# Carrying a routing gate as a 513th column of its dispatched row, in an attention and mixture-of-experts kernel

## The reference, cut to what matters

```python
probs = jax.nn.softmax(xt @ Wg, axis=-1)
gate = jnp.take_along_axis(probs, eidx[:, None], 1)[:, 0]
flat = jnp.where(keep, eidx * C + pos, E * C)
xd = jnp.zeros((E * C, d), x.dtype).at[flat].set(xt, mode='drop')
...
out = jnp.take(oe, jnp.minimum(flat, E * C - 1), axis=0)
out = out * (gate * keep.astype(x.dtype))[:, None]
out + shared
```

## Time and profile before

| | |
|---|---|
| median of 3 runs | 1058.2 us (1057.88 to 1059.21) |
| span of the profiled execution, first to last instruction | 1056.1 us |
| time of its own of that execution | not listed apart; the median stands 2.1 us above its span |
| PE busy | 1028.1 us, 97% of the span |
| DVE, ACT, POOL busy | 726.8, 551.9, 545.2 us |
| PE's share of the chain that ended last | 89% |
| granted clock of TensorE, mean | 0.996 |

### The profile page before, as it was taken

One profiled execution on the slowest core, in us unless ns is written; L12 is line 12 of the kernel. 1 busy time (PEld: TensorE's weight loads), 2 busy tenths in 40 slices (PEclk: granted clock), 3 DMA queues, 4 the chain that ended last, 5 costly groups with the idle time before them and its releaser, 6 DMA issues.

```text
span 1056.1 us, 16138 instructions
## 1 busy us (share of the span) xinstructions
PE 1028.1 (97%) x5570; PEld 720.2 (68%) x5570; DVE 726.8 (69%) x1206; ACT 551.9 (52%) x970; POOL 545.2 (52%) x309
## 2 busy tenths in 40 slices
PE   5999999999999999999999999999999999999996
PEld 5877556465564655545545568788899999998884
DVE  4549877878788788887888568723666666663164
ACT  3321565656666566665665663512455666663116
POOL 2200688988888988889888863173000000004500
PEclk9999999999999999999999999999999999999998
DMA  8945441444316253241353456372477777775604
GB/s 266 321 127 154 111 100 51 103 109 120 101 51 156 56 134 86 60 121 32 90 180 110 140 160 199 92 212 60 111 213 222 213 228 222 233 211 109 96 1 159
DMA packets 162181, 145.74 MB, mean 138 GB/s; under 512 B 42481, under 2 KB 125681, under 8 KB 161856
## 3 DMA queue, kind: packets, MB, share of 16 engines
q1 hardware_dynamic: 154720, 128.62, 43.8%
q0 software_dynamic: 6656, 15.93, 5.4%
q10 hardware_dynamic: 736, 0.30, 0.1%
HBM read 84.70 MB, written 35.67 MB: 114 GB/s over the span
## 4 chain that ended last, share of the span: by engine, by line
PE 89%; DVE 4%; DMA 2%; ACT 2%; issue 1%; SPq 0%; ACTq 0%; DVEq 0%
PE bank L829 20%; PE bank L987 13%; PE bank L1000 12%; PE bank L935 12%; PE bank L1137 10%; PE bank L923 8%; PE bank L1045 4%; PE bank L895 3%; PE bank L1012 3%; PE bank L836 2%; DVE mx L1648 1%; DMA raw<-in_L_ffn_W_dram 1%; PE bank L1114 1%; DMA lora_c<-in_L_attn_Ao_dram 1%; PE bank L868 1%
## 5 line engine op out<-in xcount | busy, mean ns | idle before, releaser
L1377 ACT ACTIVATE prob<-bank 128x512 f32<-128x512 f32 x512 | 290.1, 597 | 188.0 <-PE bank L987 180.0
L1648 DVE TENSOR_REDUCE mx<-bank 128x1 f32<-128x512 f32 x512 | 325.0, 679 | 75.4 <-PE bank L935 72.3
L758 POOL TENSOR_TENSOR psum<-psum,prob 128x1024 f32<-128x1024 f32 x156 | 366.8, 2392 | 0.0
L987 PE MATMUL bank<-Qs,Ks 97*128 97x512 f32 x512 | 208.7, 423 | 0.9 <-DMA Qs<-mrow 0.9
L935 PE MATMUL bank<-Ks,Qs 96*128 96x512 f32 x512 | 184.6, 405 | 2.9 <-DVE mx L1648 1.3
L987 PEld LDWEIGHTS bank<-Qs,Ks 97*128 97x128 f32 x512 | 94.2, 188 | 106.2 <-ACT prob L1377 74.3
L1000 PE MATMUL bank<-prob,V 128*32 128x512 f32 x1024 | 131.4, 602 | 0.0
L935 PEld LDWEIGHTS bank<-Ks,Qs 96*128 96x128 f32 x512 | 97.0, 189 | 49.3 <-DVE mx L1648 21.9
L808 POOL DMA_DIRECT2D oe_d<-oe_sb x16 | 8.7, 546 | 228.6 <-ACT oe_sb L1514 227.6
L758 POOL TENSOR_TENSOR psum<-prob,prob 128x1024 f32<-128x1024 f32 x32 | 76.1, 2399 | 62.7 <-ACT prob L1377 33.6
L923 PE MATMUL bank<-xThi,Wsl 128*128 128x512 f32 x256 | 98.4, 396 | 0.8 <-DVE plane_klo L1638 0.8
(11 more groups left out here) (257 smaller groups left out, 2075.7 us busy)
## 6 DMA issues: line engine op xcount, KB each, us to landing
raw<-in_L_ffn_W_dram SPq DMA_DIRECT2D x120, 256.0 KB, 3.6
Ks<-plane_khi SPq DMA_DIRECT2D x64, 128.0 KB, 2.5
Qs<-plane_qhi SPq DMA_DIRECT2D x64, 128.0 KB, 2.3
raw<-in_L_ffn_sw_dram SPq DMA_DIRECT2D x30, 256.0 KB, 4.0
xin<-in_L_attn_x_dram SPq DMA_DIRECT2D x16, 256.0 KB, 5.8
v_d<-v_sb POOLq DMA_DIRECT2D x16, 256.0 KB, 3.6
Ks<-plane_klo SPq DMA_DIRECT2D x32, 128.0 KB, 2.6
Qs<-plane_qlo SPq DMA_DIRECT2D x32, 128.0 KB, 2.3
```

What stands on the lines that cost most here:

```text
L758: po.tensor_tensor(psum[:, pr], (prob[0] if kc == 1 else psum)[:, pr], prob[kc % RING][:, pr], ALU.add).then_inc(sem("sum_done"), 1)
L987: nc.tensor.matmul(score_at(v, i), Ks[v.b][0:97, hh, kc * P:(kc + 1) * P], Qs[v.b][0:97, hh, v.hf * HALF:(v.hf + 1) * HALF], start=True, s ...
L1377: ACTV(prob[kc % RING][:, hh, :], score_at(v, i), ACT.Exp, scale=SCALE).then_inc(sem("exp_done"), 1)
L1648: ins = RED(mx[(hf + ahead) % 2][:, 4 * hh + qt, part:part + 1], src, AX.X, ALU.max)
```

## The change

`xd_d` gets rows of 513 elements (2052 bytes) instead of 512, and so do `rows_a` and `rows_b`. The reciprocal writes the gate into element 512 of each row, in two instructions, one for each buffer. The 16 row stores then carry the gate along; the 16 stores of gates, the table `gate_d`, its clear and two waits go. The clear of `xd_d` goes in pieces of 57 elements (228 bytes) instead of 64 (256 bytes). The slot loads read 512 of 513 elements of each row, and the gates are loaded from column 512 of `xd_d`. All users of the rows as tokens get a view of their first 512 elements. The attention stage's buffers, and with them most of the second stage's, begin 32 bytes later than before (`rows_b` now on a multiple of 64 bytes; the two `w13` buffers behind it, and everything in `late`, 64 bytes later), and the small routing buffers behind the removed gate buffer 32 bytes earlier.

```diff
+ROW = D + 1
...
-    xd_d = nc.dram_tensor("xd_d", [E * CAP, D], F32).ap()
-    gate_d = nc.dram_tensor("gate_d", [E * CAP, 1], F32).ap()
+    xd_d = nc.dram_tensor("xd_d", [E * CAP, ROW], F32).ap()
...
-    region = keep.at
+    region = keep.at + 4 * NT // 2
...
-    early = Arena(nc, region, small_at - V_BYTES)
-    rows_a = early("rows_a", [P, NT // 2, D], F32)
+    early = Arena(nc, keep.at, small_at - V_BYTES)
+    rows_a = early("rows_a", [P, NT // 2, ROW], F32)
...
-    wide = Arena(nc, overlay, sum_at)
-    rows_b = wide("rows_b", [P, NT // 2, D], F32)
+    wide = Arena(nc, overlay, sum_at + 4 * NT // 2)
+    rows_b = wide("rows_b", [P, NT // 2, ROW], F32)
...
-    late = Arena(nc, sum_at, nc.sbuf_usable_end)
+    late = Arena(nc, wide.at, nc.sbuf_usable_end)
...
     def rows(t):
+        return gated_rows(t)[:, 0:D]
+
+    def gated_rows(t):
         return (rows_a if t < NT // 2 else rows_b)[:, t % (NT // 2)]
...
-                sp.dma_start(gate_d.rearrange("(p n) o -> p (n o)", p=P), zeros[:, 0:E * CAP // P]).then_inc(sem("gate_zero"), 16)
...
-            sp.dma_start(xd_d.rearrange("(p n) (a b) -> p (n a) b", p=P, a=8)[:, i * n * 8:(i + 1) * n * 8, :],
-                         zeros[:].unsqueeze(1).to_broadcast([P, n * 8, D // 8])).then_inc(sem("xd_zero"), 16)
+            sp.dma_start(xd_d.rearrange("(p n) (a b) -> p (n a) b", p=P, a=9)[:, i * n * 9:(i + 1) * n * 9, :],
+                         zeros[:, 0:ROW // 9].unsqueeze(1).to_broadcast([P, n * 9, ROW // 9])).then_inc(sem("xd_zero"), 16)
...
-                sp.dma_start(xdi[j][:], xd_d[bass.ds(r, P), :]).then_inc(sem(f"xd_ld{j}"), 16)
+                sp.dma_start(xdi[j][:], xd_d[bass.ds(r, P), 0:D]).then_inc(sem(f"xd_ld{j}"), 16)
...
-        sp.wait_ge(sem("gate_put"), 16 * NT)
-        sp.dma_start(gate_sb[:], gate_d.rearrange("(n p) o -> p (n o)", p=P),
+        sp.dma_start(gate_sb[:], xd_d[:, D:ROW].rearrange("(n p) o -> p (n o)", p=P),
                      allow_slow_non_contiguous=True).then_inc(sem("gate_ld"), 16)
...
-                                  in_=rows(t), in_offset=None, bounds_check=E * CAP - 1,
+                                  in_=gated_rows(t), in_offset=None, bounds_check=E * CAP - 1,
                                   oob_is_err=False).then_inc(sem(f"scat{t // 4}"), 16)
-
-        po.wait_ge(sem("gate_zero"), 16)
-        for t in range(NT):
-            po.indirect_dma_start(out=gate_d, out_offset=bass.IndirectOffsetOnAxis(ap=sidx[:, t:t + 1], axis=0),
-                                  in_=r2["gate"][:, t:t + 1], in_offset=None, bounds_check=E * CAP - 1,
-                                  oob_is_err=False).then_inc(sem("gate_put"), 16)
...
-        link(nc.vector.reciprocal(r2["gate"][:], r2["sm"][:]))
+        for k, part in enumerate((rows_a, rows_b)):
+            link(nc.vector.reciprocal(part[:, :, D], r2["sm"][:, k * NT // 2:(k + 1) * NT // 2]))
```

More of the change, by code:

```diff
@@ L331, in emit @@
     r3 = {n: mid(f"r3_{n}", [P, NT, E], F32) for n in ("lg", "d", "ex", "c", "oh", "s0", "s1", "io")}
-    r2 = {n: mid(f"r2_{n}", [P, NT], F32) for n in ("mx", "sm", "gate", "em", "ps", "keep", "flat", "t")}
+    r2 = {n: mid(f"r2_{n}", [P, NT], F32) for n in ("mx", "sm", "em", "ps", "keep", "flat", "t")}
     tri = mid("tri", [P, P], BF16)
```

## The result

The changed kernel takes 1085.88 us (median of 4 runs, 1082.74 to 1089.92), the kernel before beside it 1058.04 us (4 runs, 1057.29 to 1059.21). The ratio is 1.0263, interval 1.0245 to 1.0281: slower by 27.8 us, where "no difference" was forecast and 1060.5 was the upper end.

What follows compares the result with a forecast made beforehand. PE, busy 97% of the span, was taken as the bound, the gate stores as a cost nobody pays. Six zeros and +0.1 us on the last output store took 1058.2 to 1058.3 us, "no difference"; range 1056.8 to 1060.5.

Steps and rivals of the forecast that it cites:

- The clear goes in more and odder pieces: Clear of the slot table: lands after 13 to 15 us instead of 11.3, hidden by 20.7 us of cover; 0.
- PE waiting for `Qs<-mrow`: Attention stage: with a clear of over 20.7 us, named as a sign that the forecast is wrong.
- The gate stores go: POOL, 703.45 to 724.53 us: some 21 us freed, but ScalarE sets POOL's next work; 0.
- Rival A: Gate stores disturbed something, sharing DMA engines with weight loads: 1057.0 us at best; gain over 0.2% given 0.04.
- The row stores: 16 stores of 2052 bytes a row: bytes grow 0.2%, a store may come 19 us late; 0.
- the reciprocals: DVE's chain: two of about 0.20 us, 0.18 us more in all, hidden by 0.24 us idling; 0 to +0.2.
- the gate load: Gates read from places 2052 bytes apart: landed after 4.3 us before, some 37 us of cover; 0.
- the slot loads: Expert stage, 16 loads of 256 KB at 4.5 us from rows 2052 bytes apart: a little longer is absorbed; 0.
- rival B: Expert stage: slot loads with odd starts delay each expert's weight loads; 2.1 us at 6%, 4.2 at 12%; chance 0.06.
- POOL's idle time: After POOL's last store at about 703 us: idles some 83 us instead of 62.
- the output stores: Tail: four stores, the last landing after 2.1 us; +0.1 us for the 4-byte offset, between 0 and +0.3.
- the shift by 32 bytes: All buffers, attention stage above all: engines don't mind 32 bytes; 0, with +/-1 us of uncertainty.

Runs made afterwards that it cites:

- the fourth group: Last of four groups of follow-up runs, each with the kernel before at its side; here that took 1057.4 us (21 runs), going by its time without stalls.
- three other groups: The first three groups of follow-up runs, where the kernel before took 1079.51, 1078.18 and 1078.10 us.
- the paced version: Kernel before with two waits of POOL inside its 32 indirect stores, before the first and ninth gate store: 1061.24 us, ratio 0.9839.
- the clear mended: Changed kernel with only the slot table's clear altered, to 192-byte pieces starting on multiples of 64: 1061.34 us, ratio 0.9828.
- the pauses: Two waits of POOL inside the sixteen row stores, added to the changed kernel with 192-byte clear pieces: 1057.65 us, ratio 0.9810.
- the two paced versions: Kernel before with four waits in its 32 indirect stores, 1057.32 us; changed kernel with 192-byte clear pieces and two waits in its row stores, 1057.65 us.
- the second group: Second of the four groups of follow-up runs; the kernel before took 1078.18 us there.

## Why the prediction was wrong, point by point

**"The clear goes in more and odder pieces"** is the step that failed. The mechanism was seen: no row had odd starts, the cover was 20.7 us, and PE waiting for `Qs<-mrow` was named as the sign. The size was wrong: 13 to 15 us to landing, with 0.03 for more than 20.7. It measured 43.8 us, 3.9 times the old value, and the term was not 0 but 22.0 us of waiting and 7.3 of longer PE work, most of it at the lower clock. What misled was scaling by the number of pieces (9216 to 8192): the odd starts were seen and given 2.3 us at most (15 against the 12.7 of the pieces). With no row on a resource, the only upper bound taken was the cover itself. That is a statement of what could be hidden, not of what it might cost, and it belonged in the chances at far more than 0.03. The second half of the error is that the cover was read from SP's next issue alone: a clear in flight also delays the loads beside it, on its own queue and on another (`Ks` at 17.73 us with the clear on ScalarE's).

**The clock** was in no term. The stalls of 13.9 and 8.1 us (22.0 less 13.9) each left PE at 0.50 for some 6.5 us of work, in which it lost some 3.3 us. So these two cost their length plus a quarter and two fifths, as an estimate.

**"The gate stores go", priced at 0**, was right for the trace it was read from, and in the fourth group. It wasn't in three other groups, where the run of 32 stores cost the kernel before some 17 us (1 - 0.9846 of 1078). Rival A named the place, "the 21 us of small stores did disturb something", but priced the DMA traffic of the writes and gave it 1.2 us at best. All the writes are made in the paced version too, at no cost; it is the unbroken run that hurts.

**The row stores**: landing 9.5 and 11.8 us instead of 3.9 and 3.8, not 0.2% more. The 19 us of cover held. The slots are issued at 741.73, 10.5 us behind the last store (2.9 before), and SP's next weight load at 754.25, which is where 725.16 stands after a shift of 29.1 us.

**Right as written**: the reciprocals (0.21 and 0.20 us, back to back, forecast 0.20 each), the gate load (4.6 us, hidden), the slot loads at no cost (4.7 us against 4.5, which is 4%; rival B doesn't show, as PE is busy 239.25 of the twelve windows' 240 us, before 238.66, and no wait names weights), POOL's idle time (83.45 us before its next store, forecast 83), the output stores (2.0 and 2.1 us, unchanged, so that the +0.1 of the sum doesn't show) and the shift by 32 bytes (1061 us with the clear mended in one group, 1057.65 with the pauses too, against 1057.4 in another, hold nothing against it). The sum lists seven terms for eight parts; the one left out is a zero and changes nothing.

## What to carry to other kernels

When a row in DRAM gets an odd length, look at how the table is filled, not only at who reads it: fill it flat, in pieces whose starts stay on multiples of 64 bytes, as here, or of 32, which took 15.3 us instead of 11.3, whatever the row length is. A cost that no row of the profile shows deserves a wide chance, and a cover read from one queue is not the cover of a transfer that fills all DMA engines. Break a long run of GpSimd's indirect stores with waits that the schedule meets anyway: it cost nothing in the group without stalls (0.9993) and saved 1.6% in one with them (0.9839, the gate stores paced).

## What the runs showed of the hardware

- Pieces of 256 bytes to DRAM: 4096 of them land after 6.8 us on good starts (5.3 when repeated), 7.1 at +32 or +64 bytes, 16.1 at +4. As a clear beside the attention stage, 8192 of them take 11.3 us on good starts, 15.3 at +32 and 35.0 at +4, and 9216 of 228 bytes take 43.8.
- Indirect row stores of 2052 bytes a row land 2.4 to 3.1 times later than those of 2048 (9.5 and 11.8 against 3.9 and 3.8 us; 8.4 and 9.6 against 3.9 and 3.7 in the two paced versions). Whether the length, the starts in DRAM or those in SBUF do it isn't parted.
- After stalls of 13.9 and 8.1 us TensorE worked some 6.5 us at a granted clock of 0.50, its level of 1.2 GHz, before 1.00 came back.
- A run of about 32 indirect stores of GpSimd, 1.29 us apart, can hold up ScalarE, and DVE and PE with it: it idled 19.70 and 11.66 us at two steps that had 5.85 and 3.05 in the trace without stalls. Two pauses, of 4.15 and 5.89 us, end most of that. Which resource the run takes stays open, the path of the DMA packets included. Of the loading of code, the two traces show the same single packet of 16 KB (queue q8) between 697.5 and 732 us; whether an engine waited for one isn't visible, and the path of the semaphores was not tried. Why the same kernel stalls in three groups of runs and not in two others is open too. It is not the chip alone: the second group, with stalls, and the fourth, without, bear the same chip number.
